# Spline attention: three VectorE passes over a tile, whole or one PSUM bank at a time

## The reference, cut to what matters

```python
sim = einsum('bhnd,bhdm->bhnm', q, k) / sqrt(32)
xs = clip(sim, -6, 6)
kan = base_w * silu(xs) + einsum('...k,k->...', b_splines(xs), coef)
attn = softmax(kan, axis=-1)
out = einsum('bhnm,bhmd->bhnd', attn, v)
```

## Time and profile before

| | |
|---|---|
| median of three runs | 7766.29 us (7762.79 to 7779.05) |
| the profiled execution's own time | 7772.84 us |
| its span, from the first to the last instruction | 7770.9 us |
| mean granted TensorE clock over the span | 0.960 of full |
| last layer's tile work on VectorE, first to last `add_tanh` | 2379 to 7729 us of the span, 784 tiles |
| DMA | 7 GB/s over the span |

### The profile page before, as it was taken

The page is one execution under the profiler, slowest core; times in us unless marked ns, Lnnn a source line. Parts: engine busy times, 40 slices in busy tenths (PEclk is TensorE's granted clock), DMA queues, the critical chain, the costliest instruction groups (busy, mean ns, idle before and its releaser), DMA issues. The chain is left out here.

```text
span 7770.9 us, 145982 instructions
## 1 busy us (share of the span) xinstructions
PE 6793.0 (87%) x42656; PEld 4637.1 (60%) x42656; DVE 6299.4 (81%) x9577; ACT 5760.3 (74%) x9016; POOL 5360.8 (69%) x3394
## 2 busy tenths in 40 slices
PE   5676788989977999999999999999999999999998
PEld 3454545767754666666666666666666666666666
DVE  3324175444447999999999999999999999999998
ACT  3417101222217999999999999999999999999998
POOL 3306000000007999999999999999999999999997
PEclk7878789999988999999999999999999999999999
DMA  2001000000011000000000000000000000000000
GB/s 67 22 3 39 0 0 1 0 0 0 0 35 34 1 1 1 1 1 1 11 1 1 1 1 1 1 27 1 1 1 1 1 2 2 4 4 4 4 4 6
DMA packets 75922, 55.73 MB, mean 7 GB/s; under 512 B 50776, under 2 KB 73464, under 8 KB 75032
## 3 DMA queue, kind: packets, MB, share of 16 engines
q1 hardware_dynamic: 72512, 53.88, 2.5%
q10 hardware_dynamic: 3288, 0.33, 0.0%
HBM read 37.80 MB, written 16.37 MB: 7 GB/s over the span
## 5 line engine op out<-in xcount | busy, mean ns | idle before, releaser
L1438 POOL TENSOR_TENSOR a_s<-a_s,a_v 128x784 f32<-128x784 f32 x1568 | 2912.4, 1857 | 304.1 <-ACT a_s L1649 285.7
L1474 PE MATMUL a_right_sides<-a_s,diag_d 128*128 128x392 f32 x6272 | 2280.4, 506 | 8.9 <-POOL a_s L1438 1.2
L1474 PEld LDWEIGHTS a_right_sides<-a_s,diag_d 128*128 128x128 f32 x6272 | 1130.1, 190 | 1050.2 <-POOL a_s L1438 310.7
L1570 DVE SCALAR_TENSOR_TENSOR a_kan<-a_s,spline_c,a_kan 128x784 f32<-128x784 f32 x1568 | 1622.1, 1035 | 50.4
L1497 PEld LDWEIGHTS a_weighed<-a_V,a_probT 112*128 112x128 f32 x10976 | 1374.4, 193 | 162.2
L1431 POOL TENSOR_TENSOR a_inner<-a_inner,a_x 128x784 f32<-128x784 f32 x784 | 1458.8, 1861 | 0.0
L1497 PE MATMUL a_weighed<-a_V,a_probT 112*128 112x65 f32 x10976 | 1365.3, 270 | 0.0
L1649 ACT ACTIVATE a_s<-a_v 128x784 f32<-128x784 f32 x1568 | 1335.2, 852 | 4.6
L1640 ACT ACTIVATE a_v<-a_a 128x784 f32<-128x784 f32 x1568 | 1335.7, 852 | 0.3
L1486 PE MATMUL a_turned<-ident,a_prob 128*112 128x128 f32 x5488 | 856.2, 278 | 231.9 <-ACT a_probT L1656 230.3
L1541 DVE TENSOR_SCALAR a_x<-a_scores 128x392 f32<-128x392 f32 x1568 | 876.1, 559 | 21.0 <-PE a_scores L1461 21.0
(11 more groups left out here) (181 smaller groups left out, 6858.7 us busy)
## 6 DMA issues: line engine op xcount, KB each, us to landing
rows<-bias_rows_dram SPq DMA_DIRECT2D x112, 91.0 KB
X<-in_x_dram SPq DMA_DIRECT2D x4, 1568.0 KB, 14.4
a_q<-q_dram SPq DMA_DIRECT2D x392, 16.0 KB, 2.0
mask<-in_window_mask_dram SPq DMA_DIRECT2D x56, 98.0 KB
v_dram<-V SPq DMA_DIRECT2D x14, 227.5 KB, 2.3
a_V<-v_dram SPq DMA_DIRECT2D x4, 796.2 KB, 9.2
q_dram<-Q SPq DMA_DIRECT2D x14, 224.0 KB, 1.9
k_dram<-K SPq DMA_DIRECT2D x14, 224.0 KB, 1.9
```

The costliest lines, as they stand in the source:

```text
L1438: eng.tensor_tensor(s, s, v, ALU.mult).then_inc(cubed, 1)
L1474: mm = eng.matmul(up[:, j, 0:SUB], steps[i][:, :], cubes[g][:, SUB * j:SUB * (j + 1)], start=(i == 0), stop=(i == 1))
L1570: eng.scalar_tensor_tensor(F, banked((s1, s2)[j][g][:, :]), c[:, 3 + j:4 + j], F, ALU.mult, ALU.add).then_inc(left_added, 1)
```

## The change

The three passes of steps 1 to 3 are done in halves, first bank 0 of `F`, then bank 1. Each half has a signal for its successor on the same bank: `half_tanh`, `half_based`, `half_left` for bank 0, and the old `with_tanh`, `based`, `left_added` for bank 1. `left(g, 0)` becomes `left_inner(g, j)`, `left(g, 1)` becomes `left_outer(g)` and stays one instruction. The small pieces stay between the same passes. The program has three VectorE instructions of 392 columns in two halves each where it had three of 784.

```diff
-        (loaded, q_ready, inverted, heads_folded, ...
+        (loaded, q_ready, half_tanh, half_based, half_left, inverted, heads_folded, ...
@@ -1541,33 +1541,43 @@
                         eng.tensor_scalar(x[g][:, SUB * j:SUB * (j + 1)], scp[:, j, 0:SUB], 6.0, -6.0, ALU.min, ALU.max).then_inc(clipped, 1)
                     return stage
 
-                def add_tanh(g):
+                def add_tanh(g, j):
                     def stage(eng, t, r, p):
                         n = 4 * t + g
-                        eng.wait_ge(all_added, n + 1)
-                        if g == 0:
-                            eng.wait_ge(o_ready, t + 1)
-                        eng.wait_ge(tanh_made, n + 1)
-                        eng.wait_ge(inner_made, n + 1)
-                        eng.scalar_tensor_tensor(F, S, half_base[:, :], banked(inner[g % 2][:, :]), ALU.mult, ALU.add).then_inc(with_tanh, 1)
-                    return stage
-
-                def times_x(g):
+                        if j == 0:
+                            eng.wait_ge(all_added, n + 1)
+                            if g == 0:
+                                eng.wait_ge(o_ready, t + 1)
+                            eng.wait_ge(tanh_made, n + 1)
+                            eng.wait_ge(inner_made, n + 1)
+                        eng.scalar_tensor_tensor(F[:, j, :], S[:, j, :], half_base[:, :], banked(inner[g % 2][:, :])[:, j, :],
+                                                 ALU.mult, ALU.add).then_inc((half_tanh, with_tanh)[j], 1)
+                    return stage
+
+                def times_x(g, j):
                     def stage(eng, t, r, p):
                         n = 4 * t + g
-                        eng.wait_ge(with_tanh, n + 4)
-                        eng.scalar_tensor_tensor(F, F, linear[:, :], banked(x[g][:, :]), ALU.add, ALU.mult).then_inc(based, 1)
-                    return stage
-
-                def left(g, j):
+                        eng.wait_ge((half_tanh, with_tanh)[j], n + (1, 4)[j])
+                        eng.scalar_tensor_tensor(F[:, j, :], F[:, j, :], linear[:, :], banked(x[g][:, :])[:, j, :],
+                                                 ALU.add, ALU.mult).then_inc((half_based, based)[j], 1)
+                    return stage
+
+                def left_inner(g, j):
                     def stage(eng, t, r, p):
                         n = 4 * t + g
-                        eng.wait_ge(cubed, 2 * n + j + 5)
-                        if j == 0:
-                            eng.wait_ge(based, n + 1)
-                        else:
-                            eng.wait_ge(left_added, 2 * n + 9)
-                        eng.scalar_tensor_tensor(F, banked((s1, s2)[j][g][:, :]), c[:, 3 + j:4 + j], F, ALU.mult, ALU.add).then_inc(left_added, 1)
+                        eng.wait_ge(cubed, 2 * n + 5)
+                        eng.wait_ge((half_based, based)[j], n + 1)
+                        eng.scalar_tensor_tensor(F[:, j, :], banked(s1[g][:, :])[:, j, :], c[:, 3:4], F[:, j, :],
+                                                 ALU.mult, ALU.add).then_inc((half_left, left_added)[j], 1)
+                    return stage
+
+                def left_outer(g):
+                    def stage(eng, t, r, p):
+                        n = 4 * t + g
+                        eng.wait_ge(cubed, 2 * n + 6)
+                        eng.wait_ge(half_left, n + 1)
+                        eng.wait_ge(left_added, 2 * n + 9)
+                        eng.scalar_tensor_tensor(F, banked(s2[g][:, :]), c[:, 4:5], F, ALU.mult, ALU.add).then_inc(left_added, 1)
                     return stage
 
                 def add_right(g):
@@ -1609,7 +1619,8 @@
                 for g in range(4):
                     (g2, l2), (g3, l3) = (((g - back) % 4, int(g < back)) for back in (2, 3))
                     between = {1: ([(invert, 3)], []), 2: ([], [(add_output, 4)]), 3: ([(row_max, 1)], [(negated_max, 1)])}.get(g, ([], []))
-                    order += [(add_tanh(g3), l3)] + between[0] + [(times_x(g3), l3)] + between[1] + [(left(g3, 0), l3), (clip(g, 0), 0), (left(g3, 1), l3),
+                    order += [(add_tanh(g3, 0), l3), (add_tanh(g3, 1), l3)] + between[0] + [(times_x(g3, 0), l3), (times_x(g3, 1), l3)] + between[1]
+                    order += [(left_inner(g3, 0), l3), (left_inner(g3, 1), l3), (clip(g, 0), 0), (left_outer(g3), l3),
                               (clip(g, 1), 0), (add_right(g3), l3), (gate(g2), l2)]
                 pipeline_pairs(dve, order)
```

More of the change, by code:

```diff
@@ L1362, in kan_attention3 @@
         part = lambda r, g: prob[r][:, QUART * g:QUART * (g + 1)]
-        (loaded, q_ready, inverted, heads_folded, o_ready, y_made, x_added, out_stored, margin_set, s_made, clipped, v_ready, s_ready, cubed, line_made, inner_made, tanh_made, with_tanh, based, left_added,
+        (loaded, q_ready, half_tanh, half_based, half_left, inverted, heads_folded, o_ready, y_made, x_added, out_stored, margin_set, s_made, clipped, v_ready, s_ready, cubed, line_made, inner_made, tanh_made, with_tanh, based, left_added,
          right_made, right_gated, all_added, max_found, max_ready, exp_done, turned, copied, weighed, placed, waits_met_v, waits_met_p) = (
-            sem(n) for n in ("loaded", "q_ready", "inverted", "heads_folded", "o_ready", "y_made", "x_added", "out_stored", "margin_set", "s_made", "clipped", "v_ready", "s_ready", "cubed", "line_made", "inner_made",
+            sem(n) for n in ("loaded", "q_ready", "half_tanh", "half_based", "half_left", "inverted", "heads_folded", "o_ready", "y_made", "x_added", "out_stored", "margin_set", "s_made", "clipped", "v_ready", "s_ready", "cubed", "line_made", "inner_made",
                              "tanh_made", "with_tanh", "based", "left_added", "right_made", "right_gated", "all_added", "max_found",
```

## The result

The changed kernel takes 7931.6 us (median; 7902.9 to 7942.2) against 7768.0 us before: 1.0203 times as long, 95% interval 1.0189 to 1.0218, some 164 us more. The prediction was 7906 us, slower, in a range of 7845 to 7975. The time and the direction came as predicted, but in part by luck: two terms of the sum were too large and one was missing.

A forecast was written before the change was run, and what follows sets the result against it. The prediction took VectorE's own order of slots to bound the kernel. 54 us for the halved passes plus 86 us for small pieces made +140 us on 7766, so 7906 us, in a range of 7845 to 7975.

The forecast's parts named there:

- What bounds the kernel: In the last layer's tile work VectorE's slots set the pace; 0.32 us a tile of waiting, 251 us, is all to win.
- What a half costs: A 392-column half writing PSUM: 0.407 us plus 0.131 fixed, 0.538 us; the three passes cost +54 us in all.
- What stood in the gaps: Four small pieces, free in VectorE's gaps before, now cost slots: 0.44 us a block, +86 us.
- The halves' waits at nothing: A half waits for the half two before it; 0.45 us in hand against 0.11 needed, so no cost.
- Moves on other engines: with_tanh comes 0.13 us later; TensorE's right sides keep 0.40 us in hand before gate, so nothing is lost.
- Sum: Whole kernel: 54 us for the passes plus 86 us for the small pieces, +140 us, 7906 us, 1.8% slower.
- Rivals 1: A half writing PSUM costs what a clip costs, 0.063 us less each: -157 us, 7609 us, faster; chance 0.08.
- 4: Writers of PSUM don't overlap on VectorE: halves of 0.67 us, +670 us, 8436 us; chance 0.03.
- 5: No difference in time, with VectorE half slots near 0.51 us; chance 0.04.
- 2: Small pieces still fit a VectorE gap because the halves wait a little anyway: +54 us, 7820 us; chance 0.06.
- 3: The halves' waits show on VectorE, 0.10 to 0.20 us a tile: +78 to +157 us, 7984 to 8063; chance 0.08.

The follow-up runs named there:

- The kernel with three moved pieces: Kernel before, with invert, row_max and negated_max moved from the gaps to behind the first left and first clip, add_output left in place: 7834.1 us, 1.0073.
- one wait less: Changed kernel with the wait for the cubes (cubed) taken out of left_inner and left_outer: 1.019 against the kernel before.
- the filled kernel: Changed kernel with the first transpose of every block done three times over, 0.2 us more TensorE work: 7877.1 us, 1.0128 against the kernel before.

## Why the prediction was right, and where it was not

- *What bounds the kernel.* Right: VectorE's slots, with no other engine in its waits. Its 0.32 us of gaps a tile were the most to be won, and they were won.
- *What a half costs.* Right in kind: a half that writes PSUM pays the whole fixed cost. 0.538 us was put for it and 0.533 measured. Over six halves, and with times_x no longer than the others, the passes cost 3.20 us instead of 3.233: about 30 us in all instead of 54.
- *What stood in the gaps.* Right, and the larger term: 0.39 us a block was measured for 0.44, 77 us instead of 86. The kernel with three moved pieces (37 us for 39 expected) and the one with add_tanh whole show it by itself.
- *The halves' waits at nothing.* Right: no idle before them, and one wait less brings nothing.
- *Moves on other engines: "DVE gets slower, so nothing is lost there".* This is the step that failed. It counted whether TensorE would be in time, 0.40 us in hand, and it would have been at 2.4 GHz. It did not ask what a slower pace does to TensorE's own clock. The waits cost 25 us in one profiled execution and 48 in the other; of the median they are 50 us by the filled kernel, 58 as what the slots leave of the 164.
- *Sum.* 140 us stood for 106 us of slots and 50 to 58 us of clock. The two terms of the slots were 34 us too large together, and a term of 50 to 58 us was missing; that the forecast lies only 26 us below the median is luck, the one error making up for a part of the other.
- *Rivals 1, 4 and 5* fell with the 0.53 us between two halves, 2 with the tiles of 6.98 and 6.87 us; 3 (waits that show) was wrong in place, as the new waits are gate's.

Left open: why nine stretches in one execution and seventeen in the next of the same program, why add_tanh whole, whose tiles are on average only 0.035 us shorter, has just one, and why the kernel before has none with an idle time as long as that of the kernel with three pieces moved. The stretches often come in blocks that follow one another, seven in a row from 4230 to 4415 us in the second trace of the changed kernel. The place is shown (TensorE idle for about 1 us in front of one group of scores), what decides from block to block is not.

## What to carry to other kernels

Cutting a dependent instruction in two trades the wait behind it for one more fixed cost and also closes the gap in which small work stood free; before counting a gap as loss, look at what lies in it and at why it is as long as it is: here a wait that another one already implied was the cheaper cure (0.994 against 1.020). And an engine that is second in load can still add to the time if it has idle places behind which its clock falls: here the leader's tile work became 2% longer by its slots (106 us of 5355) and 50 to 58 us more came by the clock, and one instruction of 0.2 us put 1.6 us further back cost 2.2 us a block. Before such a delay is put down to the clock, look at the blocks in which the clock stayed high: in that kernel 0.85 us of gate's wait stood there too.

## What the runs showed of the hardware that was not expected

- The kernel before runs its tile work at 2.4 GHz throughout with TensorE's idle time in front of those scores at 0.94 us. With tile work 0.7% to 2% longer and idle times of 0.94 to 1.06 us, 1 to 22 stretches of some 6.8 us at 1.2 GHz appear right behind it, each one costing about 2.8 us of the kernel's time; at 0.75 us or less and the same slots as in the changed kernel, none.
- Two waits in front of a VectorE instruction lengthen the gap behind the instruction on which it depends from 0.04 to 0.11 us; with one taken away the distance went from 1.15 to 1.08 us.
- A small VectorE instruction (1 to 4 elements a row) has a slot of 0.06 to 0.08 us, though its record is 0.15 us long.
